# A table-lookup and interaction kernel: four tiles per lookup matmul, raw tables where the low parts stand, dense features loaded features-first, and a TensorE program without a loop

## The reference

```python
e = jnp.stack([tbl_0[ids[:, 0]], ..., tbl_25[ids[:, 25]]], axis=1)
all_vecs = jnp.concatenate([dense_proj[:, None, :], e], axis=1)        # 2048 x 27 x 128
interactions = jnp.einsum('bnd,bmd->bnm', all_vecs, all_vecs)
interact_flat = interactions[:, rows, cols]                            # upper triangle, 351
z = jnp.concatenate([dense_proj, interact_flat], axis=1)
h = jnp.concatenate([z, r_dense_proj], axis=1)
h = jnp.maximum(h @ W_top1 + b_top1, 0.0)                              # 607 -> 512
h = jnp.maximum(h @ W_top2 + b_top2, 0.0)                              # 512 -> 256
y = h @ W_top3
```

## Time and profile before

| | |
|---|---|
| median of three runs | 379.75 us (379.35 to 380.21) |
| profiled execution | 379.39 us |
| its span | 377.5 us |
| TensorE matmul busy | 344.4 us (91%), 6144 records |
| TensorE weight load busy | 321.1 us (85%) |
| VectorE busy | 239.1 us (63%) |
| ScalarE busy | 143.7 us (38%) |
| GpSimd busy | 244.8 us (65%), 256 gathers |
| mean granted TensorE clock | 0.985 |

### The profile page before, as it was taken

How to read it: one execution, slowest core, us unless ns; L and a number is a source line. 1 busy time by engine, 2 the same in 40 slices (tenths; PEclk the granted TensorE clock), 3 DMA queues, 4 the chain that set the end, 5 groups by cost and what they waited for, 6 DMA issues and landing times.

```text
span 377.5 us, 14444 instructions
## 1 busy us (share of the span) xinstructions
PE 344.4 (91%) x6144; PEld 321.1 (85%) x6144; DVE 239.1 (63%) x702; ACT 143.7 (38%) x256; POOL 244.8 (65%) x260
## 2 busy tenths in 40 slices
PE   0774997979999999999999999999999999999897
PEld 0674996969988998999999998999999998998786
DVE  4989998685564876658665876658564975602300
ACT  2274331434423443525313443535413452536122
POOL 5357777777777777777777777777767777670000
PEclk9999899898999999999999999999999999999999
DMA  7999823242414232242324242232413122110000
GB/s 193 290 255 246 259 66 124 56 132 61 126 51 134 52 118 62 56 125 63 118 56 123 51 113 68 54 119 56 125 44 130 48 56 56 49 49 9 5 2 0
DMA packets 17702, 35.86 MB, mean 95 GB/s; under 512 B 6605, under 2 KB 9677, under 8 KB 17679
## 3 DMA queue, kind: packets, MB, share of 16 engines
q0 software_dynamic: 8192, 16.79, 16.7%
q1 hardware_dynamic: 8335, 18.72, 16.4%
q10 hardware_dynamic: 1152, 0.01, 0.2%
HBM read 35.49 MB, written 0.01 MB: 94 GB/s over the span
## 4 chain that ended last, share of the span: by engine, by line
PE 85%; DMA 7%; issue 2%; DVE 2%; POOL 2%; SPq 2%; ACT 0%; DVEq 0%; POOLq 0%
PE hid L395 13%; PE gram L424 12%; PE look_ps L351 8%; PE look_odd L351 8%; PE vec_act L312 8%; PE look_odd L353 8%; PE look_ps L353 7%; PE hid L402 7%; PE hid L351 4%; PE hid L353 4%; DMA vecs<-tbl,ids_sb 3%; DMA raw<-tbl 3%; POOL vecs L295 2%; PE small L414 1%; PE small L364 1%
## 5 line engine op out<-in xcount | busy, mean ns | idle before, releaser
L295 POOL DMA_INDIRECT vecs<-tbl,ids_sb x256 | 244.6, 955 | 94.6 <-issue 78.0
L572 DVE TENSOR_SCALAR onehot<-step_ids,row_no 125x256 fp32r<-125x256 int32 x640 | 196.4, 376 | 86.7 <-PE look_odd L353 38.0
L547 ACT COPY vecs_T<-vec_act 128x512 f32<-128x512 f32 x64 | 46.5, 733 | 112.1 <-PE vec_act L312 111.9
L351 PE MATMUL look_odd<-onehot,look_hi 125*128 125x256 f32 x256 | 67.9, 302 | 5.1 <-DMA vecs<-tbl,ids_sb 2.6
L351 PE MATMUL look_ps<-onehot,look_hi 125*128 125x256 f32 x256 | 67.8, 300 | 1.6 <-DVE look_lo L580 1.6
L353 PE MATMUL look_ps<-onehot,look_lo 125*128 125x256 f32 x256 | 63.7, 284 | 0.0
L353 PE MATMUL look_odd<-onehot,look_lo 125*128 125x256 f32 x256 | 63.6, 285 | 0.0
L424 PE MATMUL gram<-vecs_T 128*27 128x26 f32 x4096 | 52.4, 192 | 3.7 <-issue 1.2
L424 PEld LDWEIGHTS gram<-vecs_T 128*27 128x27 f32 x4096 | 44.1, 104 | 13.2 <-issue 6.8
L351 PEld LDWEIGHTS look_odd<-onehot,look_hi 125*128 125x128 f32 x256 | 49.2, 192 | 5.9 <-DVE look_lo L580 2.8
L351 PEld LDWEIGHTS look_ps<-onehot,look_hi 125*128 125x128 f32 x256 | 49.3, 193 | 2.2 <-DVE look_lo L580 1.8
(11 more groups left out here) (74 smaller groups left out, 288.9 us busy)
## 6 DMA issues: line engine op xcount, KB each, us to landing
step_ids<-look_ids SPq DMA_DIRECT2D x15, 640.0 KB
raw<-tbl SPq DMA_DIRECT2D x10, 448.0 KB
vecs<-tbl,ids_sb POOLq DMA_INDIRECT x256
vecs<-dense SPq DMA_DIRECT2D x16, 64.0 KB, 1.8
raw<-tbl SPq DMA_DIRECT2D x10, 52.0 KB
step_ids<-look_ids SPq DMA_DIRECT2D x1, 512.0 KB
w_sb<-w SPq DMA_DIRECT2D x1, 512.0 KB
raw<-w_dense SPq DMA_DIRECT2D x1, 512.0 KB, 10.4
```

What stands on the lines that cost most here:

```text
L295: nc.gpsimd.indirect_dma_start(out=vecs[j][:, 1 + k, :], out_offset=None, in_=tables[k], in_offset=bass.IndirectOffsetOnAxis(ap=ids_sb[:, ...
L351: nc.tensor.matmul(bank, look_hi[:, f, ch, :], onehot[:, i % SLOTS, c, :], start=ch == 0, stop=False)
L547: return engine_copy(vecs_T[j][:, :, lo:lo + GROUP], bank[:, :, :].rearrange("d v b -> d b v"))
L572: last = nc.vector.tensor_scalar(onehot[:, i % SLOTS, c, :], step_ids[a][0:LOOK_K, f - a * LOOKUPS // 2, :], row_no[0:LOOK_K, ch:ch + 1], ...
```

## The change

- A lookup matmul now covers up to four tiles, 512 columns. A unit is 2 chunks of one table, 4 matmuls; a tile's body still has 10 units, a table has 4. The ten tables fall in four classes (2, 3, 2 and 3 tables); class c is looked up for tiles 4r+c+1 to 4r+c+4 at once. The ends are narrower: in the prologue (r = -1) the classes cover 1, 2, 3 and 4 tiles; in round 3 they cover 3, 2, 1 and none. In all 47 table groups: 4 of 128 columns, 6 of 256, 4 of 384, 33 of 512, 16 matmuls each.
- ScalarE copies the first tile of a finished table straight into `vecs_T`, the other three into `looked`; `merge` moves them later, three copies a tile.
- The ids come by table and group (`wide_ids`, four slots), and each load waits until the table four places earlier has its one-hots.
- Raw tables go where their low parts will stand (`look_lo`), each in its own place, so no table load waits. VectorE takes the low part in place.
- Dense features come transposed from the host, so TensorE's `turn_dense` goes; SyncE loads them twice for each pair (`dense_new`, `dense_T`).
- The last layer has the weight column as stationary operand and 256 samples as moving one; y is one row.
- TensorE's program, and the others', are written out without a loop.
- The gates of tile 0's and tile 1's gathers count the new units: 10, 20, 30.
- TensorE no longer waits for `ident` before its first lookup.

The diff, cut to its core:

```diff
-UNIT_CH = LOOK_CH // 2
+UNIT_CH = 2
+UNITS = LOOK_CH // UNIT_CH
+IDS_SLOTS = 4
+SPAN = 4
+WIDE = SPAN * P
+CLASS_TABLES = (2, 3, 2, 3)
+CLASS_FIRST = (0, 2, 5, 7)
+PERIOD_UNITS = LOOKUPS * UNITS // SPAN
...
+    def group(r, f):
+        c = class_of(f)
+        first = SPAN * r + c + 1
+        return max(first, 0), min(first + SPAN, tiles)
...
-        raw = [sb(f"raw{k}", [P, LOOK_CH * D]) for k in range(RAWS)]
         look_hi = sb("look_hi", [LOOK_K, LOOKUPS, LOOK_CH, D], F32R)
+        with nc.sbuf_tensor("raw", [LOOK_K, LOOKUPS, LOOK_CH, D], F32) as raw:
+            pass
         look_lo = sb("look_lo", [LOOK_K, LOOKUPS, LOOK_CH, D], F32R)
...
+                def load_ids(r, f):
+                    n = number(r, f)
+                    first, end = group(r, f)
+                    if n >= IDS_SLOTS:
+                        sp.wait_ge(onehot_made, UNITS * (n - IDS_SLOTS + 1))
...
-                    if f >= RAWS:
-                        sp.wait_ge(table_split, f - RAWS + 1)
...
+                load_ids(-1, 3)
+                for f in range(3, LOOKUPS):
+                    load_table(f)
                 for f in range(4, LOOKUPS):
-                    load_table(f)
-                load_step(2, 0, 1)
+                    load_ids(-1, f)
...
                         if k % HALF_GATHERS == 0 and t < 2 and t + k > 0:
-                            pool.wait_ge(onehot_used, SLOTS * (2 * t + k // HALF_GATHERS))
+                            pool.wait_ge(onehot_used, LOOKUPS * (2 * t + k // HALF_GATHERS))
...
+                def look_up(r, f, part, count):
+                    n = number(r, f)
+                    if isinstance(r, int) and r < 0 and part == 0:
+                        pe.wait_ge(table_split, f + 1)
+                    pe.wait_ge(onehot_made, UNITS * n + part + 1)
+                    if part == 0 and positive(n - 1):
+                        pe.wait_ge(looked_up, n - 1)
+                    slot = (UNITS * f + part) % SLOTS
+                    bank = look_ps[f % 2][:, 0:count * P]
+                    for c in range(UNIT_CH):
+                        ch = part * UNIT_CH + c
+                        nc.tensor.matmul(bank, look_hi[:, f, ch, :], onehot[:, slot, c, 0:count * P],
+                                         start=ch == 0, stop=False)
+                        last = nc.tensor.matmul(bank, look_lo[:, f, ch, :], onehot[:, slot, c, 0:count * P],
+                                                start=False, stop=ch == LOOK_CH - 1)
+                    last.then_inc(onehot_used, 1)
...
-                with pe.Fori(1, pairs - 1) as r:
-                    tile(2 * r, 0, r)
-                    tile(2 * r + 1, 1, r)
+                for t in range(SPAN, tiles - 1):
+                    tile(t // SPAN, t % SPAN)
...
+                for f in range(LOOKUPS):
+                    for part in range(UNITS):
+                        make_unit(-1, f, part)
+                    take_low(f)
```

More of the change, by code:

```diff
@@ L295, in gather @@
                         nc.gpsimd.indirect_dma_start(
[L296 removed]
+                            out=vecs[j][:, k, :], out_offset=None, in_=tables[k],
                             in_offset=bass.IndirectOffsetOnAxis(ap=ids_sb[:, t, k:k + 1], axis=0),
@@ new lines, in tile @@
+                def tile(r, p, mlp=True):
+                    t, j, pair = SPAN * r + p, p % 2, 2 * r + p // 2
+                    def unit(i):
+                        f, part = unit_table(p, i)
+                        count = SPAN
+                        if isinstance(r, int):
+                            if not looked_for(r, f):
+                                return
+                            first, end = group(r, f)
+                            count = end - first
+                        look_up(r, f, part, count)
@@ L537, in _ @@
                 pe.wait_ge(h2_copied, pairs + 2)
-                for h in range(2):
-                    for c in range(H2 // P):
-                        end = nc.tensor.matmul(y_ends[1][:, h:h + 1], h2_T[:, c, h * P:(h + 1) * P], w3_sb[:, c:c + 1],
-                                               start=c == 0, stop=c == H2 // P - 1)
+                for c in range(H2 // P):
+                    end = nc.tensor.matmul(y_ends[1], w3_sb[:, c:c + 1], h2_T[:, c, :], start=c == 0, stop=c == H2 // P - 1)
                 end.then_inc(y_ready, 1)
@@ new lines, in merge @@
+                def merge(t):
+                    r, p = divmod(t - 1, SPAN)
+                    act.wait_ge(looked_up, number(r, CLASS_FIRST[p]))
+                    for k in range(1, SPAN):
+                        fs = fields_of((p - k) % SPAN)
+                        cols = slice(LOOK_COL + fs.start, LOOK_COL + fs.stop)
+                        part = nc.scalar.copy(vecs_T[t % 2][:, :, cols].rearrange("d b v -> d v b"),
+                                              looked[:, fs.start:fs.stop, k - 1, :])
+                    part.then_inc(merged, 1)
@@ new lines, in tile, with take @@
+                def tile(t):
+                    r, p = divmod(t, SPAN)
+                    n, j, pair = t + 1, t % 2, t // 2
+                    def take(i):
+                        f, part = unit_table(p, i)
+                        if part == UNITS - 1 and looked_for(r, f):
+                            take_looked(r, f)
+                    if j == 1 and pair >= 1:
+                        relu1(pair - 1, 1)
+                    copy(n, 0)
+                    take(1)
+                    copy(n, 1)
+                    if t > 0:
+                        copy_pairs(t - 1)
+                    place_dense(n)
+                    take(3)
+                    merge(n)
+                    if j == 1 and pair >= 1:
+                        relu2(pair - 1)
+                    take(5)
+                    copy(n, 2)
+                    copy(n, 3)
+                    take(7)
+                    if j == 0 and pair >= 1:
@@ L745, in tile @@
                         relu1(pair - 1, 0)
-                    if mlp and j == 1:
-                        relu2(pair - 1)
-                    unit(9)
-                    if mlp and j == 1:
+                    take(9)
+                    if j == 1 and pair >= 1:
                         result(pair - 1)
```

486 lines of the change are left out of this document (191 added, 295 removed).

## The result

| | before | after |
|---|---|---|
| median, us | 379.98 (379.35 to 380.23, 4 runs) | 396.99 (395.58 to 397.59, 4 runs) |
| profiled span, us | 377.5 | 395.7 |
| ratio to before | | 1.044, interval 1.041 to 1.047 |

Slower, as forecast, but by 17 us where I had said 2.6, and 7 us beyond the top of my range. The page of the changed kernel, busy lines, against the earlier trace rows: engine, us, share, instructions.

A forecast was written before the change was run, and what follows sets the result against it. TensorE bound the loop by 2 us a pair; afterwards GpSimd's gathers would. The prologue loses 2.4 us, 2.3 of slack goes, the end costs 2.8 more: span 380.4, plus 1.9 around it, 382.4 us, range 377 to 390.

The forecast's parts named there:

- The gather's step: GpSimd's gathers behind the last start gate: 232 at 1.255 us each, 290.9 us, the last ending at 342.0.
- the third gate: GpSimd's wait for 30 lookup units, table 8's second, behind VectorE's chain: opens at 51.1 us, bounds 49 and 54.
- the rivals: Free ids 373.8 us (0.14); quicker tables 379-380 (0.10); matmul 0.24, about 390 (0.08); stretched prologue 385-388 (0.11); starved TensorE above 400 (0.04).
- The three gates: GpSimd's waits in the prologue for 10, 20 and 30 TensorE lookup units: open at 17.7, 36.5 and 51.1 us.
- Gate 1: GpSimd's wait for 10 lookup units, table 3's second: opens at 17.7 us instead of 22.3.
- gate 2: GpSimd's wait for 20 lookup units, table 5 done: its ids, behind all ten tables, land at 29.7; opens at 36.5 us.
- The end: Behind the last gather: last turning at 344.3 us, then 33.3, 1.1 for two units, 1.7 for half clock, span 380.4.
- The 512-column matmul: TensorE's lookup step: 0.216 us for 512 columns, 0.24 at the other end, saving 1.9 us a pair or nothing.
- Written-out code: Instruction loading for TensorE's program without a loop: 0.6 us more for every pair of tiles.
- TensorE's pair: TensorE's time for two tiles in the main rounds: 40.7 us instead of 42.2, against 40.2 for GpSimd.
- One-hots of 512 columns: VectorE's prologue chain: eight one-hots of 512 columns take 5.0 us, of 384 columns 3.9.
- GpSimd bounds, and TensorE waits for it: After the change GpSimd's gathers bound the kernel and TensorE waits 4 us in tile 14's body; chance 0.53.

The follow-up runs named there:

- pieces of 256 columns: The changed kernel with each one-hot of 512 or 384 columns made by VectorE in pieces of at most 256, matmuls still wide: 387.92 us, ratio 1.021.
- the bench: Separate kernel, writing zeros: GpSimd gathers beside VectorE one-hots of several widths or ScalarE copies, then TensorE matmuls alone; gathers 0.948 us alone, one 36.51 beside 512 columns.
- early ids: The changed kernel with the ids of tables 5 to 10 issued between the table loads instead of behind all ten: 389.09 us, ratio 1.024.
- the kernel with mends: The changed kernel with ids between the tables, ScalarE splitting three tables ahead, and one-hots of at most 256 columns in the rounds only: 377.3 us, ratio 0.993.

## Why the prediction was wrong, step by step

- *The gather's step.* "232 x 1.255" is the failed step. I took the duration of the earlier trace rows as GpSimd's own. It was 1.312 (+13.1 us), since it depends on the width of what VectorE does beside it; pieces of 256 columns took 9 us back, and the bench showed the cause alone. What the pieces left, 387.9 against the 382.4 of the forecast, comes mostly from the third gate, 4.3 us later in that run than I had it, and from steps of 1.268. The prediction had priced the wide one-hots on VectorE's side only, and had no term for what they do to GpSimd. None of the rivals held it either.
- *The three gates* (17.7, 36.5, 51.1): measured 22.37, 40.23, 54.16. The mechanism was right: VectorE waited for the ids of table 5, to 32.03, where I had 29.7, and early ids took 8 us off. Gate 1 was off by 4.7: TensorE's third table waits for its low part on VectorE, whose one-hots wait for slots; I had counted the chain from a table's landing alone. It cost nothing in the end, since gate 2 waited for the ids.
- *The end.* 344.3 for the last turning, measured 359.82, which is 3.1 (gate 3) + 13.1 (steps) - 0.7 (landing 1.6 and not 2.3). Tail 36.1 with half clock, measured 35.9: right. 380.4 + 15.3 is the 395.7 of the profile. The tail is right in part by luck: it holds a stop of 2.06 us in the interactions at 375.4, for 1.18 in the earlier trace rows, which I had not added.
- *The 512-column matmul*, 0.216: measured 0.228, and 0.227 on the bench. That is midway between my two ends, 0.216 and 0.24, and with what stands around a unit the lookups of a pair gain 0.7 and not 1.9. It didn't decide this result, GpSimd being the bound; in the kernel with mends it did. The rule of the Trainium skill that I weighed (TensorE: Matmul & The Clock Gate, Back-to-back issue gap, 215.7 ns) is 12 ns too low here; the same section gives it for a matmul by itself, and has 131 ns for a stream with weight loads, which is further off.
- *Written-out code*, 0.6 a pair: nothing that the pairs show, and 1.5 us in all in the median of the program before written out. I had taken the 0.6 from one pair of rounds, and rounds that load nothing differ by as much.
- *TensorE's pair*, 40.7: 40.85 and 41.26 where it had no wait. Near, by luck: the lookups gained 1.2 us less than I had said, while the loading charge of 0.6 fell away and the interactions came out shorter than before.
- *One-hots of 512 columns*, some 0.62 in my gate 3: they start 0.40 apart on the bench, with GpSimd idle and beside it, and 0.43 in the mean in the changed kernel's prologue. Too dear, which hid part of the error of the earlier gates.
- *GpSimd bounds, and TensorE waits for it*: right, though TensorE waited for gathers eight times (12.9 us in all) and not at tile 14 alone. Of my marks, the step of 1.255 is what failed; "without a wait" held. The three waits at the gates were 9.0, 7.7 and 2.1 us, not 4.5, 9 and 4.5.

## What to carry to other kernels

When an instruction is made wider, look also at the engines that share something with its engine, and not only at its own time: here the wider VectorE instruction saved VectorE 40 us that nobody needed and cost GpSimd, the bound, 13. A duration read from a trace holds beside the work that stood there; before multiplying it by 232, ask whether the change alters that work. A loop's body and a queue's order have sizes too: a period twice as long made the body of a loop reload, by the count of packets, and ids put behind ten tables came 8 us late for the first stage.

## What the runs showed of the hardware

- GpSimd's indirect DMA (128 rows of 512 bytes, 0.94 us) can be shut out by VectorE's `tensor_scalar` from int32 to float32r for as long as that runs without a pause: 36.5 us beside 512 columns, 11 at 384, 7 at 352, each until VectorE's work ran out; nothing at 320 and below. With pauses beside 512 columns it is 1.00 to 1.08 in the mean, 1.19 for the worst.
- Beside narrow ones VectorE is the one that pays: from 0.262 to 0.311 us a one-hot at 256 columns.
- Beside a low part (`tensor_tensor`, 125 x 1024) with two one-hots of 512 columns behind it a gather took 1.99 us; no run takes the low part by itself.
- float32r matmuls with a 125-row, 128-column weight load each: 0.111, 0.120, 0.173, 0.227 us for 128, 256, 384 and 512 columns. Below 256 columns narrowing gains almost nothing; from 256 to 512 the cost per column falls by 5%.
- A TensorE loop whose body holds four tiles stopped for 4.2 us at its jump back and then ran 6.9 us at the half clock (1.2 GHz, granted 0.55); written out, the same place had no stop. Written-out code had stops of its own near the end of the program, up to 2.2 us.
